# Turning three tiles of a mixture's sums by VectorE's block transpose and transfers inside SBUF

## What is computed

```python
def _L0_cond_ref(hidden_states, gating_probs, shared_gate_prob, Wg, Wu, Wd, Sg, Su, Sd):
    h = hidden_states
    g = jnp.einsum('bsd,edf->ebsf', h, Wg)
    u = jnp.einsum('bsd,edf->ebsf', h, Wu)
    expert_outs = jnp.einsum('ebsf,efd->ebsd', jax.nn.silu(g) * u, Wd)
    expert_output = jnp.einsum('be,ebsd->bsd', gating_probs, expert_outs)
    shared = jnp.einsum('bsf,fd->bsd', jax.nn.silu(h @ Sg) * (h @ Su), Sd)
    sg = shared_gate_prob[:, :, None]
    return (1.0 - sg) * expert_output + sg * shared

def _L1_cond_ref(x, fwd_steps, T):
    Tb = T[fwd_steps - 1]
    return jnp.einsum('bij,bjk->bik', Tb, x)
x = x + _L0_cond_ref(x, fside_Bx8_0, condB_sharedgateprob[:, None], ...)
x = x + _L1_cond_ref(x, itok_B_1_98, L1_cond_T)
```

## Time and profile before

| | us |
|---|---|
| median of 3 runs | 309.67 (309.34 to 309.71) |
| the profiled execution's own time | 309.2 |
| its span, first to last instruction | 307.4 |
| TensorE busy | 303.6 |
| VectorE busy | 214.1 |
| ScalarE busy | 162.9 |
| GpSimd busy | 102.2 |

### The profile page before, as it was taken

How to read it: one execution, slowest core, us unless ns; L and a number is a source line. 1 busy time by engine, 2 the same in 40 slices (tenths; PEclk the granted TensorE clock), 3 DMA queues, 4 the chain that set the end, 5 groups by cost and what they waited for, 6 DMA issues and landing times.

```text
span 307.4 us, 4554 instructions
## 1 busy us (share of the span) xinstructions
PE 303.6 (99%) x1352; PEld 252.2 (82%) x1352; DVE 214.1 (70%) x349; ACT 162.9 (53%) x302; POOL 102.2 (33%) x116
## 2 busy tenths in 40 slices
PE   8999999999999999999999999999999999999996
PEld 7888888888888888888888888888888888888885
DVE  2766776677666666677667766777667666778784
ACT  3765555555555555555555555555555555555462
POOL 3585113441144115511551134411441155161000
PEclk9999999999999999999999999999999999999999
DMA  6600300030002000020003000003000000001332
GB/s 220 233 2 0 103 1 2 0 102 1 0 0 101 2 0 0 15 87 0 0 0 111 26 26 26 25 19 110 0 0 0 0 0 0 0 2 34 68 70 102
DMA packets 11239, 11.44 MB, mean 37 GB/s; under 512 B 4832, under 2 KB 9312, under 8 KB 11232
## 3 DMA queue, kind: packets, MB, share of 16 engines
q1 hardware_dynamic: 11232, 11.35, 11.6%
HBM read 9.77 MB, written 1.57 MB: 37 GB/s over the span
## 4 chain that ended last, share of the span: by engine, by line
PE 99%; DVE 0%; issue 0%
PE o_bank L437 11%; PE o_bank L439 11%; PE o_bank L436 11%; PE u_bank L411 11%; PE u_bank L412 11%; PE u_bank L410 11%; PE g_bank L411 10%; PE g_bank L412 10%; PE g_bank L410 10%; PE o_bank L467 1%; PE o_bank L460 1%; PE g_bank L474 0%; PE u_bank L474 0%; DVE res L352 0%; PE g_bank L460 0%; PE u_bank L449 0%
## 5 line engine op out<-in xcount | busy, mean ns | idle before, releaser
L323 DVE TENSOR_TENSOR u_bank<-u_bank,silu_g 128x512 f32<-128x512 f32 x144 | 100.7, 700 | 84.1 <-PE u_bank L412 83.3
L264 ACT ACTIVATE silu_g<-g_bank 128x512 f32<-128x512 f32 x144 | 86.1, 598 | 134.3 <-PE g_bank L412 133.4
L329 DVE TENSOR_TENSOR h_lo<-u_bank,h_hi 128x512 fp32r<-128x512 f32 x144 | 98.0, 681 | 0.1
L243 POOL TENSOR_TENSOR acc<-acc,scaled 128x512 f32<-128x512 f32 x32 | 41.4, 1293 | 163.2 <-DVE scaled L337 163.1
L270 ACT ACTIVATE h_hi<-u_bank 128x512 fp32r<-128x512 f32 x144 | 85.5, 593 | 0.7 <-DVE u_bank L323 0.7
L436 PE MATMUL o_bank<-h_hi,w_hi 128*128 128x512 f32 x144 | 56.1, 390 | 0.0
L439 PE MATMUL o_bank<-h_lo,w_hi 128*128 128x512 f32 x144 | 56.0, 389 | 0.0
L437 PE MATMUL o_bank<-h_hi,w_lo 128*128 128x512 f32 x144 | 56.0, 389 | 0.0
L411 PE MATMUL u_bank<-x_lo,w_hi 128*128 128x512 f32 x143 | 55.6, 389 | 0.0
L410 PE MATMUL u_bank<-x_hi,w_hi 128*128 128x512 f32 x143 | 55.6, 389 | 0.0
L412 PE MATMUL u_bank<-x_hi,w_lo 128*128 128x512 f32 x143 | 55.6, 389 | 0.0
(11 more groups left out here) (61 smaller groups left out, 145.1 us busy)
## 6 DMA issues: line engine op xcount, KB each, us to landing
w_raw<-in_W_all SPq DMA_DIRECT2D x8, 768.0 KB, 4.4
T_plus<-in_TT SPq DMA_DIRECT2D x16, 64.0 KB, 1.7
out_y<-res SPq DMA_DIRECT2D x3, 256.0 KB, 2.2
acc<-in_xT SPq DMA_DIRECT2D x2, 256.0 KB, 3.4
acc<-in_xT SPq DMA_DIRECT2D x1, 512.0 KB, 6.2
turned_y<-yB SPq DMA_DIRECT2D x2, 256.0 KB, 2.3
y<-turned_y SPq DMA_DIRECT2D x8, 64.0 KB, 2.3
w_raw<-in_W_gu SPq DMA_DIRECT2D x1, 384.0 KB, 4.0
```

Of the source, the lines that this page charges most:

```text
L243: nc.gpsimd.tensor_tensor(acc[:, t, :], acc[:, t, :], scaled[:, t % 2, :], ALU.add).then_inc(acc_done, 1)
L264: nc.scalar.activation(silu_g[:, k % 2, :], g_bank[k % 2][:, :], ACT.Silu).then_inc(g_read, 1)
L323: nc.vector.tensor_tensor(u_bank[k % HR][:, :], u_bank[k % HR][:, :], silu_g[:, k % 2, :], ALU.mult).then_inc(h_done, 1)
L329: nc.vector.tensor_tensor(h_lo[:, k % HR, :], u_bank[k % HR][:, :], h_hi[:, k % HR, :].bitcast(F32), ALU.subtract).then_inc(split_done, 1)
```

## The change

The buffer in memory is no longer used. Tiles 0 to 2 are turned by VectorE's transpose of blocks and by 16 transfers a tile from `yB` to `y`, inside SBUF: one for each 32 by 32 block, for the four samples of the tile at once (32 partitions by 4 by 32 numbers, 16 KB). SP issues all 16 for tiles 0 and 1. For tile 2 SP issues the 8 of the upper two rows of blocks, and ScalarE the 8 of the lower two, between `silu(143)` and `round_h(142)`. The four sums of tile 2 and its transpose stand together on VectorE ahead of `make_h(142)`. `turn_y(2)` and `copy_y(2)` go. On TensorE `step_y(1)` now stands ahead of down 141, and down 141, 142 and 143 stand together behind it. `step_y(2)` waits for the transfers.

```diff
-        yB = sb("yB", [P, 2, W])
+        yB = sb("yB", [P, NT - 1, W])
...
-        MOVED = 2
-        TURN_BLOCKS = [N_ROUTED + NC * t + NC + LAG + 1 for t in range(MOVED)]
+        MOVED = NT - 1
+        TURN_BLOCKS = [N_ROUTED + NC * t + NC + LAG + 1 for t in range(MOVED - 1)]
...
+        def move_block(queue, t, q, i):
+            rows, columns = slice(q * Q, (q + 1) * Q), slice(i * Q, (i + 1) * Q)
+            queue.dma_start(y[rows, t * BT:(t + 1) * BT, columns],
+                            yB[columns, t, :].rearrange("p (b f) -> p b f", b=BT)[:, :, rows]).then_inc(y_in[t], 16)
...
             for t in range(MOVED):
                 sp.wait_ge(yB_done, t + 1)
-                sp.dma_start(z[t, :, :, :].rearrange("b p f -> p b f"),
-                             yB[:, t, :].rearrange("p (b f) -> p b f", b=BT)).then_inc(z_out, 16)
-                sp.wait_ge(z_out, 16 * (t + 1))
-                for q in range(P // Q):
-                    sp.dma_start(y[q * Q:(q + 1) * Q, t * BT:(t + 1) * BT, :].rearrange("p b (i c) -> p (b i) c", c=Q),
-                                 z[t, :, :, q * Q:(q + 1) * Q].rearrange("b (i p) c -> p (b i) c", p=Q)).then_inc(y_in[t], 16)
+                for q in range(P // Q if t < MOVED - 1 else P // Q // 2):
+                    for i in range(P // Q):
+                        move_block(sp, t, q, i)
...
             for n in range(N_ROUTED + PEEL_ACT, N + 1):
                 if n < N:
                     silu(n, n)
+                if n == N - 1:
+                    act.wait_ge(yB_done, MOVED)
+                    for q in range(P // Q // 2, P // Q):
+                        for i in range(P // Q):
+                            move_block(act, MOVED - 1, q, i)
                 round_h(n - 1, n - 1)
-            copy_y(NT - 2)
...
-                if n in (SCALE_2, SCALE_2 + 1):
+                if n == SCALE_2:
                     dve.wait_ge(o_done, E * NT + NT - 1)
-                    for b in range(2):
-                        add_shared((NT - 2) * BT + 2 * (n - SCALE_2) + b)
+                    for j in range(BT):
+                        add_shared((NT - 2) * BT + j)
+                    dve.wait_ge(yT_done, BT * MOVED)
+                    nc.vector.transpose(yB[:, MOVED - 1, :], yT[:, MOVED - 1, :]).then_inc(yB_done, 1)
...
                 if i < MOVED:
-                    pe.wait_ge(y_in[i], 64)
+                    pe.wait_ge(y_in[i], 16 * (P // Q) ** 2)
...
-                for d in {N - 2: [], N - 1: [N - 4, N - 3]}.get(n, [n - LAG]):
+                for d in {N - 2: [], N - 1: [N - 4]}.get(n, [n - LAG]):
                     project_down(d, d)
             pe.wait_ge(g_read, N - 1)
             step_y(1)
-            turn_y(NT - 2)
-            project_down(N - 2, N - 2)
-            project_down(N - 1, N - 1)
+            for d in range(N - 3, N):
+                project_down(d, d)
             step_y(NT - 2)
```

More of the change, by code:

```diff
@@ L22, in moe_then_step_kernel @@
     TT: bass.AP,
-    z: bass.AP,
     out: bass.AP,
@@ L84, in moe_then_step_kernel @@
         yB_done = sem("yB_done")
-        z_out = sem("z_out")
-        y_in = [sem(f"y_in{t}") for t in range(2)]
+        y_in = [sem(f"y_in{t}") for t in range(NT - 1)]
         late_done = sem("late_done")
@@ L273, in copy_y @@
                 b, nb = parts[i]
-                act.wait_ge(y_turned, i - 1)
+                act.wait_ge(y_turned, i - NT + 2)
                 nc.scalar.activation(y[:, b:b + nb, :], part_bank(i)[:, 0:nb * D].rearrange("p (b d) -> p b d", b=nb),
@@ L455, in step_y @@
                 if i < MOVED:
-                    pe.wait_ge(y_in[i], 64)
+                    pe.wait_ge(y_in[i], 16 * (P // Q) ** 2)
                 else:
-                    pe.wait_ge(y_done, i - 1)
+                    pe.wait_ge(y_done, i - NT + 2)
                 for j in range(nb):
@@ L567 @@
         args.append(nc.dram_tensor(f"in_{name}", a.shape, _mybir.dt.from_np(a.dtype), kind="ExternalInput").ap())
-    args.append(nc.dram_tensor("turned_y", (2, 4, P_, P_), _mybir.dt.float32, kind="Internal").ap())
     args.append(nc.dram_tensor("out_y", (S_, B_, D_), _mybir.dt.float32, kind="ExternalOutput").ap())
```

## The result

The changed kernel takes **320.74 us** (median of 4, 318.96 to 322.03), the kernel before on the same chip 309.69 (309.34 to 309.71). The ratio is 1.0357, with a 95% interval of 1.0337 to 1.0377: slower by 11.05 us, seven times the forecast 1.56 and outside the stated range. The profiled execution is the fastest of the four, 318.96, with a span of 317.0.

The account below looks back on a forecast made before the run. The prediction took TensorE's instruction stream plus a short tail as the bound. Tile 0, tile 1 and the reordering at 0 each, plus 1.56 for ScalarE's held rounding, gave 309.67 + 1.56 = 311.2 us, range 309.8 to 313.6.

Parts of the forecast that it names:

- What bounds the kernel: Whole kernel: as long as TensorE's instruction stream plus a short tail, TensorE busy 99% of the span at full clock.
- The price of one issue: SP and ScalarE queues: 0.39 us from issue to issue on SP, 0.43 on ScalarE, high end 0.53.
- Tile 0, "covered, by 0.7 us only": Ahead of step_y(0): 16 SP issues land at 289.2, before TensorE asks at 289.87, so cost 0.
- Rival 1: Both queues issue slowly, 0.53 us apart: tile 0 late by 1.4, ScalarE's hold +2.4, together +3.8, 313.4 us; chance 0.20.
- Tile 1, "SP is free at 287.9": Ahead of step_y(1): SP's moves start at 289.77 and land at 297.3, before TensorE asks at 298.48, so cost 0.
- Tile 2, ScalarE, "+1.56": ScalarE's 8 issues take 3.44 us ahead of round_h(142), so the last down product starts at 303.21 instead of 301.65: +1.56.
- Landing, 1.7: Block transfers: 1.7 us from issue to landing, from the T_plus row, with 2.3 as the high end.
- VectorE's stretch: Tile 2 on VectorE: sums together from 295.88, transpose for 0.71, yB ready at 297.74; the later split still covered.
- The reordering, 0: TensorE: step_y(1) moved ahead of down projection 141 costs 0 by itself.
- "The tail keeps its shape": Behind step_y(2): turning and stepping tile 3 and the last stores add 0.
- Rival 3, the clock: TensorE near the end: a pause costs the full clock level, 2.3 us more, 313.5 us; chance 0.04.
- The Trainium skill's rule against many small transfers: All 48 transfers: coalesce, since under 64 KB one pays mostly overhead; the sum charged only those delaying a rounding.

Follow-up runs that it names:

- the run with the pauses filled: The changed kernel with products of zeros on TensorE in its three pauses, all transfers and waits kept: 317.43 us, against 309.49 for the kernel before.
- The first probe: The kernel before with 54 extra SP transfers, nine forms six times each, in the stretch where SP only waits: 309.89 us, against 309.44.
- tile 2 alone: The kernel before with only tile 2 moved by block transfers, 8 issues each on SP and ScalarE; tiles 0 and 1 through memory: 314.68 us, ratio 1.0173.

## Why the prediction was wrong

**What bounds the kernel** was read rightly: all of the eleven us are TensorE waiting or running at a lower clock.

**The price of one issue is the step that failed.** It took the row nearest in number of pieces (0.345) and from there 0.39 and 0.43 from issue to issue, with 0.53 as the high end. Measured: 0.643 on SP and 0.652 on ScalarE. Number of pieces was the wrong measure of nearness, and hardly matters (0.59 for 32, 0.60 for 128, 0.64 for 512). What all rows read had in common was memory on one side, which the prediction does not mention; the new transfers have none, and no row of the kernel before has that form. So neither end was a bound, and the high end least of all. The estimate for ScalarE was half right in kind: it costs what SP costs, and 0.02 more.

**Tile 0, "covered, by 0.7 us only", cost 0.** At 0.643 the 16th block starts at 291.75 and lands 1.83 later, at 293.6: 3.3 of wait. Rival 1 had this mechanism with 1.4.

**Tile 1, "SP is free at 287.9", cost 0.** SP was not free before 292.4. That is a failure of its own beside the size: each tile was costed from the moment its blocks were ready, and the queue's backlog was looked at once, with the cheap price. 40 issues of 0.64 are 25.9 us, where SP had from 281.6 to about 299.6 if step 2 was not to wait. Wait ahead of step 1: 1.8, which here lies inside the stretch that the held rounding would have cost anyway.

**Tile 2, ScalarE, "+1.56".** The place and the mechanism were right: eight issues, then the rounding, 5.25 us of idle `<-issue`. Mis-sized was the term 8 x 0.43 = 3.44; it was 5.35. With the measured prices the prediction's own sum gives the waits: blocks of tile 2 ready 3.3 late by tile 0's wait, at 301.0, and 0.3 more in this execution, which ran late from the start: 301.3, where they were ready at 301.46. With 5.35 of issues the rounding starts at 306.7 (306.89) and, 2.00 behind it, the last product at 308.7 (309.08). Without the 0.3 that is +6.8 before any clock.

**Landing, 1.7:** measured 1.8. **VectorE's stretch** was right: the transpose ran at 300.75, 1.15 behind the first sum, as foreseen (1.15). **The reordering, 0:** right within 0.56. **"The tail keeps its shape"** was wrong by 2.2 us in the profiled execution: 1.3 at the lower clock, 0.8 in the last store.

**Rival 3, the clock (0.04),** came true on top of the rest and not instead of it. The pauses were priced at 1.6 us "at most", since the issue was; they came to 3.3, 1.8 and 1.9 us. It cost about 3.1 us, to within 1, by the run with the pauses filled. Its price (2.3) was near, partly by luck, since it was worked out for one pause and there were three; its chance was far off, because it hung on the length of a pause that hung on the failed term. The Trainium skill, "TensorE: Matmul & The Clock Gate", section "Part 1: The HAM clock gate (the "warmup" mystery)", has the array's clock halved when it has stood idle; the runs agree, 0.50 behind a pause of 3.2 and 1.00 with that pause filled. Not each pause did it: in the profiled execution of the changed kernel the one of 3.2 us left the clock at 1.00, and it fell behind the two of 1.6 and 1.7 us.

**The Trainium skill's rule against many small transfers** ("DMA: Bandwidth & Descriptors", section "Rules for kernel authors") deserved a larger share: the prediction quoted it and charged only the issues that delay a rounding. The first probe shows it plainly: 4 KB and 256 KB take 0.59 and 0.60 to issue. The same page's sentence that an issue is usually small beside the transfer (section "Issuing engines are not separate DMA queues") does not hold here: 0.60 of 1.8 to landing, and with 40 in a row only the issue counts.

## What to carry to other kernels

When a change swaps a few large transfers for many small ones, multiply the count by the price of issues back to back of that very pair of memories, and lay all of them end to end on the queue, backlog included, before looking at any single deadline. If no row of the trace has the same source and destination, measure it: extra transfers in a stretch where the queue idles hardly change the kernel's time (309.53 with 21 of them and 309.89 with 54, one execution each, against 309.5 and 309.4). A pause on TensorE may be followed by a stretch at half clock, which counts in full where nothing behind it waits, and next to nothing where the next wait covers it.

## What the runs showed of the hardware that was not expected

- The issue of a transfer costs more when source and destination are of the same kind: 0.33 us single and 0.43 back to back from memory to SBUF, 0.47 and 0.60 from SBUF to SBUF, 0.49 and 0.59 from memory to memory, all in flat forms of 128 rows. The change's own form took 0.75 as the first of its six and 0.60 behind that.
- A store from SBUF to memory right behind a transfer from SBUF to SBUF took 0.59 to issue, the store behind it 0.41.
- Size and number of pieces hardly matter to SBUF-to-SBUF issues: 0.59 for 4 KB in 32 pieces, 0.60 for 256 KB, 0.64 for 512 pieces.
- SP and ScalarE issuing at once hardly slow each other: 0.60 and 0.62 each, against 0.60 for SP alone and 0.64 for ScalarE's last issue in the run with its issues behind the roundings, when SP issued nothing. Only where both began together (tile 2 alone) did SP's second issue take 0.79, where it took 0.61 with SP alone.
- A pause of 3.2 us on TensorE was followed by the lower clock level in one kernel and not in another with the same pause. Executions of the changed kernel vary by 3.1 us, the slowest with the lowest clock (0.978) and the fastest with the highest (0.993).
